# Gated slot attention block on one core: first weights in quarters, low-rank product per chunk, K and V projections together, output and gate projections together

## The reference

```python
q = rope(hs @ Wq.T); k = rope(hs @ Wk.T); v = hs @ Wv.T; g = hs @ Wg.T
s = clip(hs @ Ws1.T @ Ws2.T + bs2, -32, 32)          # Ws1: 16 x 512, Ws2: 1024 x 16
z = cumlogsumexp(s over time); es = exp(s); enz = exp(-z)
A  = tril(q @ k.T * scale)
ok = enz * (A @ es);  qv = softmax(ok)
W2 = tril((qv * enz) @ es.T);  o = W2 @ v
o_g = o * rsqrt(mean(o*o) + eps) * g_norm_weight * silu(g)
x = layernorm(x + o_g @ Wo.T)
out = layernorm(x + x @ (ffn_w * scale).T + bias)
```

## Time and profile before

| what | value |
|---|---|
| median of 3 runs | 1505.05 us |
| profiled execution | 1506.76 us, of which the span (first to last instruction) is 1504.1 us |
| PE busy | 1461.3 us (97%) |
| PEld busy | 1187.4 us (79%) |
| DVE busy | 906.9 us (60%) |
| ACT busy | 518.7 us (34%) |
| POOL busy | 503.1 us (33%) |
| granted TensorE clock, mean | 0.996 |

### The profile page before, as it was taken

One profiled execution on the slowest core, in us unless ns is written; L12 is line 12 of the kernel. 1 busy time (PEld: TensorE's weight loads), 2 busy tenths in 40 slices (PEclk: granted clock), 3 DMA queues, 4 the chain that ended last, 5 costly groups with the idle time before them and its releaser, 6 DMA issues.

```text
span 1504.1 us, 22717 instructions
## 1 busy us (share of the span) xinstructions
PE 1461.3 (97%) x9072; PEld 1187.4 (79%) x9072; DVE 906.9 (60%) x1616; ACT 518.7 (34%) x995; POOL 503.1 (33%) x445
## 2 busy tenths in 40 slices
PE   7999999999999999999999999999999999999988
PEld 3788888887788888887788888888788888887766
DVE  4555656566665656555765655556665565656667
ACT  5333323234332323333332333223433322323346
POOL 2423323332332333224233322423332242333245
PEclk9999999999999999999999999999999999999999
DMA  8311112022211202112420211112221111212123
GB/s 296 108 48 39 59 46 74 28 98 95 74 59 46 74 24 74 47 39 80 137 74 24 74 46 39 58 47 95 87 102 46 40 59 46 74 37 68 64 86 124
DMA packets 51413, 106.55 MB, mean 71 GB/s; under 512 B 5360, under 2 KB 15600, under 8 KB 46960
## 3 DMA queue, kind: packets, MB, share of 16 engines
q1 hardware_dynamic: 49008, 100.95, 20.0%
q10 hardware_dynamic: 2304, 4.20, 0.7%
HBM read 82.84 MB, written 22.28 MB: 70 GB/s over the span
## 4 chain that ended last, share of the span: by engine, by line
PE 82%; POOL 5%; DVE 5%; ACT 4%; issue 2%; DMA 2%; POOLq 0%; DVEq 0%; SPq 0%; ACTq 0%
PE bank_kg L863 23%; PE bank_qv L863 19%; PE bank_a L863 11%; PE bank_t L877 7%; POOL o_gated L446 4%; PE bank_wo L1061 4%; PE bank_a L898 3%; PE bank_e L890 3%; PE bank_wo L1036 3%; PE bank_wo L977 2%; PE bank_c L1066 2%; DMA w_raw<-w_groups 1%; ACT w_hi L477 1%; POOL rms L444 1%; PE bank_wo L1040 1%
## 5 line engine op out<-in xcount | busy, mean ns | idle before, releaser
L444 POOL TENSOR_TENSOR rms<-var,minus_half 128x4 f32<-128x4 f32 x64 | 65.3, 1020 | 620.9 <-DVE var L829 620.9
L863 PE MATMUL bank_qv<-w_hi,hs_hi 128*128 128x512 f32 x512 | 208.6, 407 | 2.7 <-DVE w_lo L632 2.7
L863 PE MATMUL bank_kg<-w_hi,hs_hi 128*128 128x512 f32 x512 | 207.7, 406 | 1.0 <-DVE rope_b L652 1.0
L863 PE MATMUL bank_qv<-w_hi,hs_lo 128*128 128x512 f32 x512 | 203.3, 397 | 0.0
L863 PE MATMUL bank_qv<-w_lo,hs_hi 128*128 128x512 f32 x512 | 202.6, 396 | 0.0
L863 PE MATMUL bank_kg<-w_hi,hs_lo 128*128 128x512 f32 x512 | 202.6, 396 | 0.0
L863 PE MATMUL bank_kg<-w_lo,hs_hi 128*128 128x512 f32 x512 | 201.8, 394 | 0.0
L414 POOL TENSOR_TENSOR k_rot<-rope_a,rope_b 128x512 f32<-128x512 f32 x64 | 82.4, 1288 | 207.7 <-DVE rope_b L652 207.7
L686 DVE RECIPROCAL enzT<-cumsT 128x256 f32<-128x256 f32 x64 | 112.2, 1753 | 63.5 <-ACT cumsT L521 49.6
L477 ACT ACTIVATE oT_hi<-bank_t 128x512 fp32r<-128x512 f32 x65 | 39.0, 599 | 264.1 <-PE bank_t L877 264.1
L410 POOL TENSOR_TENSOR q_rot<-rope_a,rope_b 128x512 f32<-128x512 f32 x64 | 82.5, 1289 | 111.0 <-DVE rope_b L652 111.0
(11 more groups left out here) (173 smaller groups left out, 3072.0 us busy)
## 6 DMA issues: line engine op xcount, KB each, us to landing
w_raw<-w_groups SPq DMA_DIRECT2D x32, 1024.0 KB, 5.0
x_scratch<-part SPq DMA_DIRECT2D x65, 256.0 KB, 2.0
hs_raw<-hs_cols SPq DMA_DIRECT2D x64, 256.0 KB, 2.9
part<-x_scratch SPq DMA_DIRECT2D x49, 256.0 KB, 2.8
batch_raw<-hs_cols SPq DMA_DIRECT2D x4, 1024.0 KB, 8.1
u_part<-u_scratch SPq DMA_DIRECT2D x64, 64.0 KB, 2.6
part<-hs_rows SPq DMA_DIRECT2D x16, 256.0 KB, 3.0
w_raw<-x_scratch SPq DMA_DIRECT2D x16, 256.0 KB, 2.7
```

What stands on the lines that cost most here:

```text
L444: pool.tensor_tensor(rms[:, :], var[:, :], minus_half[:, :], ALU.pow).then_inc(rms_made, 1)
L863: mm = pe.matmul(dst, x, y, start=start and n == 0, stop=stop and n == 2, **kw)
```

## The change

What it does:

1. Prologue: no batch loads. The first chunk of hs comes first, then the first WQ in four quarters of 256 KB, `ws1`, the tables, WK in quarters; WV and WG quarters follow as the raw buffer comes free. ScalarE and VectorE split quarter by quarter (`first_hi`, `first_lo`), and TensorE projects quarter by quarter (`first_project`). The memsets go, all but one, and a small ScalarE copy stands ahead of the first load.
2. `u` is made per chunk from `hs_raw` (4 fp32 matmuls of 128x128) in the prologue and in steps 1 to 15, between the oT transposes and the K projection, and kept in SBUF for all groups (`u_all`); its store and loads go.
3. Step order on TensorE: V projection directly after K; output product directly after the slot scores, ahead of the `prob` transposes; G projection directly after these; then W2, `turn_and_sum`, the `k_rot` transposes, o.
4. The dummy output of step 1 goes; the output of chunk i - 1 is worked in step i, and nothing in step 1.
5. Weight splits: WQ stays after `eps_sum` in the step c = 2, now ahead of `pT`; WK's low part goes to GpSimd, after `es_split` of that step; WV's is halved, around `rotate_q`, `okT` and `oT_lo` in the step c = 3; WG's stays after `eps_sum` in the step c = 3. `scale_ffn` and `split_ffn` move to the place after `eps_sum`.
6. `make_enz` moves from behind `mask_w2` to behind `mask_a`, ahead of `wo_lo`. On ScalarE the q copy stands ahead of the exponential, and the tanh of the gate ahead of `turned`.
7. Tiles that shared memory with the batch buffers get their own.

```diff
+            load_hs(0, 0)
+            for k in range(KT):
+                load_first(WQ, k)
             sp.dma_start(ws1_raw[:, :], ws1).then_inc(ws1_in, 16)
+            sp.dma_start(small[:, 0:TABLE_COLS], small_in[:, 0:TABLE_COLS]).then_inc(const_in, 16)
+            for k in range(KT):
+                load_first(WK, k)
+            for k in range(KT):
+                sp.wait_ge(first_lo_made, KT * WQ + k + 1)
+                load_first(WV, k)
+            sp.dma_start(small[:, TABLE_COLS:], small_in[:, TABLE_COLS:]).then_inc(ws2_in, 16)
             load_hs(1, 1)
+            for k in range(KT):
+                sp.wait_ge(first_lo_made, KT * WK + k + 1)
+                load_first(WG, k)
+            sp.wait_ge(first_lo_made, KT * WG + KT)
             load_w(WO, 0)
...
                 if left:
                     k_sum((c + 1) % 2, done(u, c, 1))
                     es_split((c + 1) % 2, done(u, c, 1))
+                    if last and c == 2:
+                        pool.wait_ge(w_hi_made, g * 4 + 2)
+                        pool.tensor_tensor(w_lo[WK][:, :], w_raw[SLOT[WK]][:, :], w_hi[WK][:, :].bitcast(F32),
+                                           ALU.subtract).then_inc(wk_lo_made, 1)
...
+                if last and c == 3:
+                    w_split(WV, next_raw_in(WV, g))
+                if i > 1:
+                    from_bank(oT_hi, bank_t[:, :], oT_mm, i - 1, oT_hi_made)
+                if n <= CHUNKS:
+                    u_hi(n)
                 if last and c == 2:
                     act.wait_ge(q_mm, n)
                     w_split(WQ, next_raw_in(WQ, g))
                 if last and c == 3:
                     w_split(WG, next_raw_in(WG, g))
                 if left:
                     from_bank(qT[:, :], bank_t[:, :], qT_mm, n, qT_made)
+                act.wait_ge(ok_shifted, i)
+                act.activation(prob, prob, ACT.Exp).then_inc(prob_made, 1)
+                if left:
                     exp_s((c + 1) % 2, n)
                     from_bank(v[(c + 1) % 2][:, :], bank_qv[:, :], v_mm, n, v_made)
                 if last and c == 2:
                     w_split(WK, next_raw_in(WK, g))
...
                 if left:
-                    turned((c + 1) % 2, n, c == CB - 1)
-                    if last and c == 2:
-                        w_split(WV, next_raw_in(WV, g))
                     act.wait_ge(g_mm, n)
                     act.activation(gate[(c + 1) % 2][:, :], bank_kg[:, :], ACT.Tanh, scale=0.5).then_inc(th_made, 1)
+                    turned((c + 1) % 2, n, c == CB - 1)
                     from_bank(kT[:, :], bank_t[:, :], kT_mm, n, kT_made)
...
+                if last and c == 3:
+                    w_split_half(WV, g * 4 + 3, 0)
                 if left:
                     rotate_q((c + 1) % CB, n)
...
-                lo(oT_lo[:, :], bank_t[:, :], oT_hi[:, :], oT_hi_made, i, oT_lo_made)
+                if i > 1:
+                    lo(oT_lo, bank_t[:, :], oT_hi, oT_hi_made, i - 1, oT_lo_made)
+                if n <= CHUNKS:
+                    u_lo(n)
+                if last and c == 3:
+                    w_split_half(WV, g * 4 + 3, 1)
+                if left:
+                    rotate_k((c + 1) % CB, n)
...
-                dve.wait_ge(pT_mm, i)
-                dve.tensor_tensor(pT[:, :], bank_t[:, 0:H], enzT[:, :], ALU.mult).then_inc(pT_made, 1)
-
                 if last and c == 2:
-                    w_split(WQ, g * 4 + 5)
+                    w_split(WQ, g * 4 + 1)
                 if last and c == 3:
-                    w_split(WG, g * 4 + 8)
+                    w_split(WG, g * 4 + 4)
+                if left == CB - 1:
+                    scale_ffn()
+                if left == CB - 2:
+                    split_ffn()
...
+                dve.wait_ge(pT_mm, i)
+                dve.tensor_tensor(pT[:, :], bank_t[:, 0:H], enzT[:, :], ALU.mult).then_inc(pT_made, 1)
...
-                if last and c == 2:
-                    w_split(WK, g * 4 + 6)
-                if left:
-                    make_enz((c + 1) % 2, n)
+                if left:
                     make_gate((c + 1) % 2, n)
...
                 if left:
                     mask_a(n)
+                    make_enz((c + 1) % 2, n)
                 if c == 0:
                     dve.wait_ge(wo_hi_made, u + 1)
                     dve.scalar_tensor_tensor(wo_lo[:, :], w_raw[0][:, :], gn, wo_hi[:, :].bitcast(F32),
                                              ALU.mult, ALU.subtract).then_inc(wo_lo_made, 1)
-                if last and c == 2:
-                    w_split(WV, g * 4 + 7)
-                if left == CB - 1:
-                    scale_ffn()
-                if left == CB - 2:
-                    split_ffn()
...
+            def low_rank(slot):
                 for k in range(KT):
-                    mm = pe.matmul(per_head((bank_a if b % 2 else bank_s)[:, :], CB), ws1_raw[:, P * k:P * k + P],
-                                   batch_raw[b % 2][:, :].rearrange("p (c k t) -> p c k t", c=CB, k=KT)[:, :, k, :],
+                    mm = pe.matmul(u_acc, ws1_raw[:, P * k:P * k + P], hs_raw[slot][:, P * k:P * k + P],
                                    start=k == 0, stop=k == KT - 1)
                 mm.then_inc(u_mm, 1)
+            def first_project(m, dst):
+                for k in range(KT):
+                    pe.wait_ge(first_lo_made, KT * m + k + 1)
+                    mm = product(dst[:, :], cols((hs_hi[0], hs_lo[0]), P * k, P), cols((w_hi[m], w_lo[m]), F * k, F),
+                                 start=k == 0, stop=k == KT - 1)
+                return mm
...
+                if i > 1:
+                    pe.wait_ge(o_norm_made, i - 1)
+                    transposes(o_gated).then_inc(oT_mm, 1)
+                if n <= CHUNKS:
+                    low_rank(nxt)
...
 
                     pe.wait_ge(gate_made, i)
                     if last and c == CB - 1:
-                        w_ready(g * 4 + 6)
+                        pe.wait_ge(wk_lo_made, g + 1)
                     project(WK, bank_kg, nxt).then_inc(k_mm, 1)
+                    pe.wait_ge(q_turned, n)
+                    if last and c == CB - 1:
+                        w_ready(g * 4 + 3, g * 3 + 2)
+                    project(WV, bank_qv, nxt).then_inc(v_mm, 1)
                     pe.wait_ge(q_summed, n)
...
                 if left:
-                    pe.wait_ge(u_in[nxt], (u * 2 + ((c + 1) // 2 + 1)) * 16)
-                    pe.matmul(slots_acc, u_part[nxt][:, :], ws2_cols(g, last and c == CB - 1), start=True,
+                    if last and c == CB - 1:
+                        pe.wait_ge(ws2_made, 6)
+                    u_cols = slice(P * (i % CHUNKS), P * (i % CHUNKS) + P)
+                    pe.matmul(slots_acc, u_all[:, u_cols], ws2_cols(g, last and c == CB - 1), start=True,
                               stop=True).then_inc(s_mm, 1)
...
-
-                    pe.wait_ge(q_turned, n)
-                    if last and c == CB - 1:
-                        w_ready(g * 4 + 7)
-                    project(WV, bank_qv, nxt).then_inc(v_mm, 1)
-                pe.wait_ge(prob_made, i)
-                if left:
-                    pe.wait_ge(qT_made, n)
-                else:
-                    pe.wait_ge(oT_lo_made, i)
-                transposes(prob, HG // 2).then_inc(pT_mm, 1)
-
-                for h in range(HG):
-                    mm = product(bank_a[:, :], cols((oT_hi, oT_lo), P * h, P), cols((wo_hi, wo_lo), D * h, D),
-                                 start=h == 0, stop=h == HG - 1)
-                mm.then_inc(out_mm, 1)
+                if i > 1:
+                    pe.wait_ge(oT_lo_made, i - 1)
+                    for h in range(HG):
+                        mm = product(bank_a[:, :], cols((oT_hi, oT_lo), P * h, P), cols((wo_hi, wo_lo), D * h, D),
+                                     start=h == 0, stop=h == HG - 1)
+                    mm.then_inc(out_mm, 1)
+
+                pe.wait_ge(prob_made, i)
+                if left:
+                    pe.wait_ge(qT_made, n)
+                transposes(prob, HG // 2).then_inc(pT_mm, 1)
+                if left:
+                    pe.wait_ge(k_turned, n)
+                    if last and c == CB - 1:
+                        w_ready(g * 4 + 4, g * 3 + 3)
+                    project(WG, bank_kg, nxt).then_inc(g_mm, 1)
...
                 if left:
                     pe.wait_ge(cumsT_made, 2 * i)
                     turn_and_sum(nxt, n)
-
-                    pe.wait_ge(k_turned, n)
-                    if last and c == CB - 1:
-                        w_ready(g * 4 + 8)
-                    project(WG, bank_kg, nxt).then_inc(g_mm, 1)
                     pe.wait_ge(k_summed, n)
                     transposes(k_rot[nxt]).then_inc(kT_mm, 1)
                 if not left:
```

337 lines of the change are left out of this document (153 added, 184 removed).

## The result

The kernel after takes 1495.37 us (median of 4 runs, 1494.26 to 1497.03), the kernel before 1506.19 in the same series (1504.58 to 1508.19). The ratio is 0.9928, with a 95% interval of 0.9911 to 0.9946: faster by 0.7%. The forecast was 1490, with 1482 to 1501 for 8 in 10. The span of the profiled execution fell from 1504.1 to 1493.2, by 10.9; the forecast for it was -15.3.

The account below looks back on a forecast made before the run. TensorE was taken to set the time, so only its waits could yield gains. Terms -16.4 + 13.7 - 1.7 - 3.2 - 5.6 - 4.0 + 1.9 = -15.3 gave 1490 us, with 1482 to 1501 for 8 in 10.

Parts of the forecast that it names:

- step 1's first Q: Sign that the forecast is right: step 1's first Q projection starts at 28 to 31 us.
- the lower clock beyond 20 us: Sign that the forecast is wrong, pointing to rival C: TensorE at its lower clock beyond 20 us.
- rival C: Prologue gains only 12 through lower clock and ScalarE's serialising order, no gain at group changes: 1500; chance 0.12.
- prologue: Start to step 1's first Q: quartered loads and splits let step 1 start at 29.5 instead of 45.87, -16.4 (-19 to -12).
- group changes: Steps c = 2 and c = 3 there: 2.0 too much a change against 3.85, three times, -5.6 (-8 to 0).
- low-rank product, 15 steps: Steps 1 to 15: four fp32 matmuls on TensorE's path, 0.91 each step, +13.7 (12 to 16).
- dummy output: Step 1: 12 matmuls and four transposes go, but the exponential's wait is uncovered, -1.7 (-3.2 to -1).
- c = 1: Steps c = 1: reciprocal ahead of `wo_lo` removes the 0.20 wait for `o_gated`, 16 times, -3.2 (0 to -3.2).
- last steps: End of the kernel: waits of 1.49 and 1.00 go, 1.51 is covered, -4.0 in all (-6 to -1.5).
- mask to o: Every step, mask of W2 ahead of o: 0.1 to spare, 0.03 a step allowed, +1.9 (0 to +10).
- rival A: Reciprocal holds GpSimd up all the same, `o_gated` 0.9 late in 16 steps c = 0: +14, 1504; chance 0.08.
- wait for `w_lo` of about 1.5 ahead of G: Sign of being right: at a group change's c = 3, G waits about 1.5 for WG's low part.

Follow-up runs that it names:

- fill: combined plus 15 unused matmuls in TensorE's prologue pauses, 6 ahead of the first q transposes and 9 ahead of G: 1482.99 us, ratio to before 0.9849.
- combined: The better mixture with the edits of the prologue kernel and of tail added: 1484.50 us, ratio to before 0.9864.
- prologue kernel: Kernel after with the `u` copies behind the WK quarters on ScalarE and VectorE, and GpSimd's `hs_lo` of chunk 2 behind `es_lo`: 1492.17 us, one run.
- lock_back: Kernel after with `wo_lo` ahead of the reciprocal again in the 16 steps c = 0: 1494.69 us, one run.
- wg_quarters: Kernel after with WG's low part at group changes made in four passes, G waiting quarter by quarter: 1489.95 us, one run.
- The two delays: Kernel after with an unused VectorE reduce ahead of the mask of W2, long (0.41 us) or short: 1517.28 and 1497.07 us, one run each.
- tail: Kernel after with the reciprocal ahead of the mask of the scores in step 63 only: 1492.50 us, one run.
- the better mixture: Kernel after with the old TensorE order in step 1, c = 2 and c = 3, the new in c = 0, c = 1 and the last step: 1485.99 us.
- delay_short: Kernel after with a small unused VectorE reduce (128 x 16) ahead of the mask of W2: 1497.07 us, one run.

## Why the prediction was right, and where its sizes were off

The direction, the range and the main mechanisms held. Two of the signs that I named did not: step 1's first Q came at 33.66, not at 28 to 31, and the lower clock beyond 20 us, the sign of rival C, did show. C's half on the prologue (-12) is what came; its other half, no gain at the group changes, did not. So the total lies where it does because the prologue came out near its worst bound while the group changes gave more than said. Against the forecast's terms, in us of the span:

| term | forecast | measured |
|---|---|---|
| prologue | -16.4 | -12.2 |
| low-rank product, 15 steps | +13.7 | +13.4 (0.89 a step, against the same kind of step later in the same kernel) |
| dummy output | -1.7 | -1.6 (step 1: -0.73, with the low rank's +0.89 in it) |
| c = 1 | -3.2 | -2.8 |
| group changes | -5.6 | -6.5 |
| last steps | -4.0 | -2.1 |
| mask to o, and the rest by difference | +1.9 | +0.9 |
| sum | -15.3 | -10.9 |

The failing term is the prologue: 4.2 too little gained, where the whole span fell 4.4 short. By the chain's own links, 0.85 of this had come up by V's end and 4.5 by G's. Three steps of it, each in the rows above:

- "the other three at VectorE's pace of some 0.65" and "V, whose quarters are split meanwhile": I had priced two-operand quarters at 0.69 with nobody beside them. The rule of the shared port was in the same prediction, applied to `o_gated`; I didn't run it over the prologue, where `q_rot`, `hs_lo`, `k_rot` and `es_lo` all stand against `w_lo`. 4.66 and 3.99 instead of 2.5 each. G's 1.5 is on the path whole. Of V's 2.2 only a part is: VectorE was through with V's quarters at 22.2, and the slot scores that it needed next came at 23.15. How much, no run shows.
- "The slot scores follow, the clip, and only then VectorE's WG quarters: G ends at 26". VectorE also splits the slot weights and rotates k ahead of the clip (22.23 to 24.0), which I had left out. WG's quarters started at 24.29, and G started on its first at 26.08.
- The clock. I took the upper level from K on and put the lower one into the bound. It came back on G, where it cost about 1.6 (six projection matmuls at 0.43 instead of 0.23, and four of 0.21 instead of 0.12). fill, without it, reached step 1 1.5 earlier than combined, which had it on G.

That ScalarE's `u` copy stands ahead of WK was in the forecast, at its right size; in the prologue kernel K starts 1.9 earlier without it.

Right by its own steps: Q at 6.26 (6.5 said); the low-rank product at nearly the price of `scores` (0.89 against 0.91), on the path, and without the 0.15 for a change between fp32 and fp32r that the upper bound allowed, which no run shows; the dummy; c = 1, by the reciprocal standing between the mask and `wo_lo`, shown from both sides (1.04 and 3.02 in lock_back) and its 0.18 a step returned when undone; rival A is out by the same rows. The "wait for `w_lo` of about 1.5 ahead of G" is 1.27 idle and 1.53 from start to start, the short one ahead of V 0.35 (0.5 said), and wg_quarters removes two thirds of the 1.85 that such a step has too much. A change costs 1.95 now, where 2.0 was said. The group changes gained 0.9 more than said because the forecast took the first change's 3.85 of before for all three; the second and third had cost 4.4 and 4.1.

Too wide, without harm: "0.1 to spare" at o. The two delays and the weight loads give 0.04. In the kernel after the mask costs nothing at o, so the 0.03 a step that I allowed for it were not paid there. The 0.02 that c = 2 and c = 3 are longer stands ahead of the `k_rot` transposes already. The other 0.06 in c = 3 was forecast to cost nothing: ScalarE's k copy comes behind `turned` (826.43 its end), and `scores` starts 1.06 behind o instead of 0.99. Steps c = 0 are 0.05 shorter.

The last steps: the three old waits went as said. What I missed is that the reciprocal's new place also lies in front of `tick`'s statistics: I followed what the move does to `o_gated`, and not who else stands behind it on VectorE in the one step where the last phase begins. The tail kernel undoes it in part (2.73 to 1.28, with 1.1 more at `okT`). Nor did the 0.8 come that I expected from half the low clock period: the low stretch lies over the same output product as before.

What remains open: why one step (45, a c = 0 one) is 0.29 longer than its like in every new kernel, what decides in which execution the tail has a low clock stretch (lock_back and tail have none, all other kernels have one), and how the prologue's 4.2 divide between the shared operands and the clock.

The best of the kernels, fill, takes 1482.99, the kernel after 1495.37. They ran on different occasions, each with the kernel before beside it (1506.22 and 1506.19). The ratios to that are 0.9849 (0.9833 to 0.9865) and 0.9928 (0.9911 to 0.9946).

## What to carry to other kernels

When an instruction is priced from a row, ask what ran beside that row, and what will run beside it in its new place: a pass of 0.69 alone was 1.2 to 1.8 against GpSimd. When one order is exchanged for another throughout a loop, tabulate the steps by kind for both and ask of each product what it covers; here no single order was the best, and the better mixture has a sum of steps of 1351.3 against 1353.8 and 1358.4. The medians differ by more, 5.5 and 9.4 (1485.99 against 1491.52 and 1495.37), and the rest is the last stretch and where the prologue's low clock fell. To learn how much room a chain has, delay it by a known amount and read the step, not the wait: a weight load can be late while the matmul behind it starts on time (0.03 late in delay_short, with the first matmul of o at 1.56 as before).

## What the runs showed of the hardware that was not expected

- The same prologue, instruction for instruction, ended at 31.53 to 35.88 in nine profiled executions. The lower clock level (matmuls of 128x512 at 0.43 from start to start instead of 0.23) stood from 27.95 to 31.36 in the kernel after, from 18.63 to 22.04 before. By an estimate from these distances it costs up to 1.6, and less where a wait hides it; the rest of the spread is when TensorE leaves the lower level at the start. So the span of a single run can't tell 3 us from nothing, while the lengths of like steps repeat to 0.02.
- Filling TensorE's pauses with 15 unused matmuls went with no such stretch in the one profile of it, and the first Q of step 1 came 1.5 earlier than in combined.
- TensorE's first matmuls, from 6.26 to 10.5, also stand 0.42 apart, though the granted clock shows 1.00 over 5 to 10: the trace's first record of the clock begins at 10.88, so at the very start the column doesn't tell the pace, the distances do.
